# Expert 0's first 256 rows picked by one-hot products, four weight parts moved to GpSimd, and a re-timed order

## What is computed

```python
x = x + tanh(g_xattn[0]) * L0_xattn(layernorm(x), ctx)
x = x + tanh(g_ffn[0])   * L0_ffn(layernorm(x))
x = x + tanh(g_xattn[1]) * L1_xattn(layernorm(x), ctx)
x = x + tanh(g_ffn[1])   * L1_ffn(layernorm(x))
# L1_ffn: 896 tokens, 8 experts, top 2
probs = softmax(x @ gate_w.T); w, idx = top_k(probs, 2); w = w / sum(w)
for each expert e:  g, u = split(x @ gup[e].T)
                    out += combine[:, e] * ((silu(g) * u) @ dn[e].T)
```

## Time and profile before

| what | value |
|---|---|
| time, median of 3 runs (lowest, highest) | 584.78 us (584.68, 585.03) |
| profiled execution, device time | 583.47 us |
| its span, first to last instruction | 581.6 us |
| PE busy | 555.4 us (95%) |
| DVE busy | 408.8 us (70%) |
| ACT busy | 319.4 us (55%) |
| POOL busy | 271.9 us (47%) |
| mean granted TensorE clock | 0.995 |

### The profile page before, as it was taken

One profiled execution on the slowest core, in us unless ns is written; L12 is line 12 of the kernel. 1 busy time (PEld: TensorE's weight loads), 2 busy tenths in 40 slices (PEclk: granted clock), 3 DMA queues, 4 the chain that ended last, 5 costly groups with the idle time before them and its releaser, 6 DMA issues.

```text
span 581.6 us, 13614 instructions
## 1 busy us (share of the span) xinstructions
PE 555.4 (95%) x5542; PEld 477.1 (82%) x5542; DVE 408.8 (70%) x831; ACT 319.4 (55%) x632; POOL 271.9 (47%) x237
## 2 busy tenths in 40 slices
PE   8999999999989999999999999998999999999994
PEld 8776667677657878888888888877899999979994
DVE  7877568578696666777767867767677677746652
ACT  3554555555664665566555556654465656636641
POOL 3755655765740164657567465731203233421424
PEclk9999999999999999999999999999999999999998
DMA  8910840000000000000000000019374567726112
GB/s 259 357 45 2 318 194 3 1 3 2 2 2 1 2 1 2 8 9 17 18 9 18 10 25 1 25 26 414 91 253 149 170 213 253 259 32 236 28 20 26
DMA packets 24091, 50.92 MB, mean 88 GB/s; under 512 B 7072, under 2 KB 17104, under 8 KB 20688
## 3 DMA queue, kind: packets, MB, share of 16 engines
q1 hardware_dynamic: 18560, 45.20, 21.4%
q0 software_dynamic: 4224, 3.70, 3.6%
q10 hardware_dynamic: 1232, 1.01, 0.6%
HBM read 37.89 MB, written 13.31 MB: 88 GB/s over the span
## 4 chain that ended last, share of the span: by engine, by line
PE 81%; DVE 7%; ACT 5%; POOL 4%; issue 2%; DMA 1%; POOLq 0%; DVEq 0%; ACTq 0%
PE ps L59 15%; PE ps L60 14%; PE ps L61 14%; PE ps L607 5%; PE ps L750 4%; PE ps L625 4%; PE ps L768 4%; PE ps L738 4%; ACT P L1642 3%; DVE KN L1140 3%; PE ps L641 3%; PE ps L515 2%; PE ps L816 2%; POOL P L1947 2%; PE ps L522 2%
## 5 line engine op out<-in xcount | busy, mean ns | idle before, releaser
L1947 POOL TENSOR_SCALAR P<-P,rinv 112x487 f32<-112x487 f32 x56 | 88.2, 1588 | 50.9 <-DVE rinv L1183 50.7
L1140 DVE TENSOR_REDUCE KN<-ps 112x4 f32<-112x1500 f32 x32 | 55.0, 1719 | 28.7 <-PE ps L607 28.6
L424 POOL DMA_INDIRECT out<-WS,rows_i x16 | 28.7, 1791 | 92.5 <-ACT WS L1789 89.0
L60 PE MATMUL ps<-XGf,WH 128*128 128x256 f32 x252 | 71.3, 283 | 0.0
L61 PE MATMUL ps<-XGf,WL 128*128 128x256 f32 x252 | 71.3, 283 | 0.0
L59 PE MATMUL ps<-XGf,WH 128*128 128x256 f32 x252 | 71.3, 283 | 0.0
L1886 POOL TENSOR_TENSOR sr<-sv,mhalf 125x32 f32<-125x32 f32 x13 | 70.7, 5435 | 1.1
L1521 DVE TENSOR_TENSOR WL<-WR,WH 128x1024 fp32r<-128x1024 f32 x48 | 57.1, 1219 | 13.6 <-ACT WH L1843 10.0
L1642 ACT ACTIVATE P<-ps 125x1344 f32<-125x1344 f32 x32 | 41.3, 1292 | 32.8 <-PE ps L625 32.8
L1705 ACT ACTIVATE P<-ps,nm 112x487 f32<-112x487 f32 x64 | 41.9, 664 | 31.7 <-DVE nm L1175 31.7
L1843 ACT ACTIVATE WH<-WR 128x1024 fp32r<-128x1024 f32 x48 | 48.7, 1049 | 0.1
(11 more groups left out here) (290 smaller groups left out, 1546.1 us busy)
## 6 DMA issues: line engine op xcount, KB each, us to landing
WR<-in_gupT SPq DMA_DIRECT2D x16, 1024.0 KB, 7.2
WR<-in_dwnT SPq DMA_DIRECT2D x8, 1024.0 KB, 10.3
xs<-ZT SPq DMA_DIRECT2D x14, 516.0 KB, 6.0
CT<-in_ctxT SPq DMA_DIRECT2D x1, 2250.0 KB, 11.1
P<-xs SPq DMA_DIRECT2D x7, 256.0 KB, 10.8
P<-xs SPq DMA_DIRECT2D x9, 128.0 KB, 2.6
Wk<-in_L_xattn_Wk SPq DMA_DIRECT2D x2, 512.0 KB, 11.1
Wv<-in_L_xattn_Wv SPq DMA_DIRECT2D x2, 512.0 KB, 11.1
```

Of the source, the lines that this page charges most:

```text
L60: e.matmul(out, ah, bl, start=False, stop=False)
L1140: e.tensor_reduce(heads(KN[b % 2][0:NQ, 3, :])[:, 4 * k:4 * k + 4, 16], ps[0:NQ, 0:4, 0:NC], AX.X, ALU.max, negate=True).then_inc(s("smax" ...
L1947: e.tensor_scalar(P[:, k, 0:487], P[:, k, 0:487], rinv[:, k:k + 1], None, ALU.mult).then_inc(s("psc"), 1)
```

## The change

Three things are changed.

Expert 0's first 256 rows no longer come from the list in device memory. For each sequence b a matrix PG of 112 tokens x 256 slots is made that holds a one where the token chose expert 0 and stands in that slot. GpSimd makes it for sequences 0 to 6 (stage "pk": a copy of `chosen`, then an is-equal of the slot numbers with `r_u`, times the copy), VectorE for sequence 7, in one operation in the middle of its "rt5". TensorE multiplies XN by PG (stage "pa": two products of 256 columns in full float32 for each sequence, accumulated over the eight in banks 0 and 1); what stands there then is the turned rows. The stage "xin" of expert 0 is only its copy and subtraction now. The two loads of expert 0's rows and the wait for the stores in front of them are gone; SyncE's first load behind the stores is expert 1's. The stores themselves remain, since the other experts and the weights use the list.

The low parts of chunks 0 to 3 of expert 0 are made by GpSimd, those of chunks 4 and 5 as before by VectorE. ScalarE makes all six high parts before it copies the last sequence's turned tokens.

The tables are re-timed, `WARM` is changed, and "xin" of expert 1 stands behind the fourth up unit of expert 0, not the third. The gates' four small operations in sequence 7's chain stand behind the product and the pick.

Of the diff, tables are cut to a line or two:

```diff
+PICK = ((1.67, "pk", 0), (1.95, "pk", 1), (3.34, "pk", 2), (14.8, "pk", 3), (20.7, "pk", 4), (29.03, "pk", 5),
...
-WARM = {("kp", 0, 1, 0): 36, ("spk", 0, 2): 24, ("xt", NB - 1, 3): 18, ("rt4", NB - 1): 26, ("xin", 0): 62,
-        ("up", 0, 0): 10}
+WARM = {("kp", 0, 1, 0): 36, ("spk", 0, 2): 24, ("xt", NB - 1, 3): 18, ("rt4", NB - 1): 10, ("pa", NB - 1): 8,
+        ("up", 0, 0): 8}
...
-            if dc == 2 and x + 1 < NE:
+            if dc == (2 if x else 3) and x + 1 < NE:
                 put("xin", x + 1)
...
+                elif stage == "pa":
+                    b, = i
+                    if b == 0:
+                        w.wait_ge(s("prob"), 2 * NPAIR)
+                    if b < NB - 1:
+                        w.wait_ge(s("pk"), 2 * b + 2)
+                    else:
+                        w.wait_ge(s("picked"), 1)
+                    for k in range(2):
+                        t = e.matmul(ps[:, PAIRS[0][k], 0:256], XN[:, b, k * 128:(k + 1) * 128], PG[:, b, :],
+                                     start=(b == 0), stop=(b == NB - 1))
+                    if b == NB - 1:
+                        t.then_inc(s("xin"), 1)
...
                 at = c + 14
+                if b == NB - 1:
+                    w.wait_ge(s("slots"), 2)
+                    w.wait_ge(s("rchain"), c + 10)
+                    e.scalar_tensor_tensor(PG[:, b, :], slots, r["u"][:, 0:1], chosen[:, b, 0:1].to_broadcast([NQ, 256]),
+                                           ALU.is_equal, ALU.mult).then_inc(s("picked"), 1)
+                    gates(e, w, b, c + 10)
...
-            w.wait_ge(s("scatter"), 32 * NB)
-            for c in range(LATE_LOW, 4):
-                split_low(e, w, 0, c)
...
         def split_low(e, w, x, c):
             cs = slice(c * 1024, (c + 1) * 1024)
             w.wait_ge(s("wh"), 6 * x + c + 1)
+            if (x, c) == (0, 4):
+                w.wait_ge(s("wl"), 4)
...
-            w.wait_ge(s("scatter"), 32 * NB)
-            e.dma_start(XG[:, 1, :], xs[128:256, 0:D]).then_inc(s("xg_first"), 16)
...
+                    e.iota(slots_i, pattern=[[1, 256]], base=0, channel_multiplier=0).then_inc(s("slots"), 1)
+                    w.wait_ge(s("slots"), 1)
+                    e.tensor_copy(slots, slots_i).then_inc(s("slots"), 1)
+                elif stage == "low":
+                    split_low(e, w, *i)
+                elif stage == "pk":
+                    b, = i
+                    w.wait_ge(s("slots"), 2)
+                    w.wait_ge(s("rchain"), RC * b + 14)
+                    e.tensor_copy(R["p2"][:, b, 0:1], chosen[:, b, 0:1]).then_inc(s("pk"), 1)
+                    w.wait_ge(s("pk"), 2 * b + 1)
+                    e.tensor_scalar(PG[:, b, :], slots, R["u"][:, b, 0:1], R["p2"][:, b, 0:1], ALU.is_equal,
+                                    ALU.mult).then_inc(s("pk"), 1)
```

More of the change, by code:

```diff
@@ L142 @@
[L142 to L156, removed]
+EVEN = ((-5.7, "xs1"), (-3.48, "q1", 0), (0.86, "q1c", 0), (3.9, "q1", 1), (5.62, "q1c", 1), (9.87, "k1x", 0),
+        (11.53, "k1xc", 0), (19.54, "k1x", 1), (21.65, "k1xc", 1))
@@ new lines @@
+ODD = ((6.06, "x1c"),)
+PREP1 = ((-6.82, "cs1"), (2.23, "k1", 0), (3.37, "k1c", 0), (2.36, "k1", 1), (5.44, "k1c", 1), (7.38, "k1", 2),
+         (10.55, "k1c", 2), (14.97, "k1", 3), (19.62, "k1c", 3), (19.17, "v1", 0), (18.96, "v1c", 0),
+         (18.89, "v1", 1), (18.58, "v1c", 1), (21.07, "v1", 2), (31.38, "v1", 3), (22.32, "v1c", 2),
+         (33.18, "v1c", 3))
+TAIL1 = ((9.54, "aT"), (13.09, "wo"), (14.24, "res", 3), (14.89, "stats", 3), (16.88, "norm", 3), (20.86, "xt", 3),
+         (19.19, "xtc", 3), (24.49, "rt0"), (21.04, "rt1"), (22.74, "rt2"), (24.47, "rt3"), (27.75, "rt4"),
+         (29.34, "rt5"))
@@ new lines @@
+TAIL_NEXT = ((8.16, "aT"), (12.94, "wo"), (9.94, "res", 3), (21.65, "stats", 3), (22.44, "norm", 3),
+             (25.94, "xt", 3), (24.18, "xtc", 3), (28.72, "rt0"), (30.67, "rt1"), (32.04, "rt2"), (34.39, "rt3"),
+             (55.11, "rt4"), (67.44, "rt5"))
+TAIL_LAST = ((3.1, "rv"), (6.19, "rb"), (4.0, "rbc"), (9.29, "aT"), (9.5, "wo"), (13.18, "res", 3),
+             (14.76, "stats", 3), (27.06, "norm", 3), (28.36, "xt", 3), (47.6, "xtc", 3), (48.16, "rt0"),
+             (48.03, "rt1"), (48.15, "rt2"), (54.71, "rt3"), (54.17, "rt4"), (77.95, "rt5"))
@@ new lines @@
+SPLIT = ((12.04, "split", 0), (21.0, "low", 0), (14.07, "split", 1), (21.32, "low", 1), (21.02, "split", 2),
+         (53.34, "low", 3), (24.66, "split", 3), (36.38, "low", 2), (25.92, "split", 4), (32.12, "split", 5))
+PICK = ((1.67, "pk", 0), (1.95, "pk", 1), (3.34, "pk", 2), (14.8, "pk", 3), (20.7, "pk", 4), (29.03, "pk", 5),
+        (29.24, "pk", 6), (22.54, "pa", 0), (24.2, "pa", 1), (37.14, "pa", 2), (51.21, "pa", 3), (61.73, "pa", 4),
+        (62.6, "pa", 5), (81.66, "pa", 6), (84.72, "pa", 7))
@@ L217, in attention_order @@
         at(d, stage, k)
+    for d, stage, b in PICK:
+        at(pair_at[NPAIR - 4] + d, stage, b)
     for d, stage, c in SPLIT:
@@ L233, in expert_order @@
             put("load", x, c)
-    put("pair", 0)
+    put("pair", 1)
     put("ahead", 0)
-    put("pair", 1)
     for c in range(3):
@@ L402, in build @@
         below, every = PF[0:NQ, 4736:4864], PF[0:NQ, 4864:4992]
+        slots = PF[0:NQ, 4736:4992]
         tri, ones = sb("tri", [NQ, 128], BF), sb("ones", [NQ, 128], BF)
@@ L858, in tensor_experts @@
                 keep_warm(e, w, stage, *i)
-                if stage == "xin":
+                if stage == "xin" and i[0]:
                     x, = i
@@ L864, in tensor_experts @@
                         w.wait_ge(s(f"pair{u % 3}"), u // 3)
+                    w.wait_ge(s(f"xg{j}"), 16 * ((x + 1) // 2))
                     for t_ in range(2):
[L866 to L869, removed]
                         for k in range(2):
@@ L940, in tensor_experts, with rows_in, rows_to @@
                         w.met.pop()
+        def rows_in(x):
+            if x == 0:
+                return ps[:, 0:2, 0:256]
+            return ps[:, PAIRS[pair_use[("xin", x)] % 3][0], :].rearrange("p (k n) -> p k n", k=2)
+        def rows_to(x, v):
+            return XGT[:, x % 2, v, :].rearrange("p (k n) -> p k n", k=2)
         def counts(e, w):
@@ L1385, in vector_route @@
             elif stage == "rt4":
[L1386 to L1392, removed]
+                if b < NB - 1:
+                    gates(e, w, b, c + 9)
             else:
@@ L1412, in vector_route, with gates @@
                     at += 3
+        def gates(e, w, b, at):
+            v2, s1, s2 = (r1[n][:, b:b + 1] for n in ("v2", "s1", "s2"))
+            e.tensor_scalar(s1, v2, 1.0, None, ALU.add).then_inc(s("rchain"), 1)
+            w.wait_ge(s("rchain"), at + 1)
+            e.reciprocal(s2, s1).then_inc(s("rchain"), 1)
+            w.wait_ge(s("rchain"), at + 2)
+            e.tensor_scalar(XN[:, b, D:D + 1], s2, tg[0:NQ, 3:4], None, ALU.mult).then_inc(s("rchain"), 1)
+            e.scalar_tensor_tensor(XN2[b][:, D:D + 1], v2, s2, tg[0:NQ, 3:4], ALU.mult,
+                                   ALU.mult).then_inc(s("rchain"), 1)
         def first_of(e, w, at, eq, mx, oh):
```

28 lines of the change are left out of this document (10 added, 18 removed).

## The result

The changed kernel takes 595.98 us (median of 4 runs, 594.94 to 596.49), the kernel before 584.89 us (4 runs beside them): ratio 1.0192, 95% interval 1.0180 to 1.0204. It is 11.1 us slower, where 4.05 us less had been forecast. The profiled execution took 596.49 us, the slowest of its four, its span is 594.7 us, TensorE's mean granted clock 0.986; so the two traces lie 13.1 us apart (594.7 - 581.6) where the medians lie 11.1 apart.

What follows compares the result with a forecast made beforehand. TensorE bounds the kernel, but a store-and-load chain through other engines sets the first gate; TensorE's queue replaces it. -4.6 + 0.35 + 0.2 = -4.05 us: profiled 583.47 becomes 579.4, median 580.7, range 579.1 to 582.3 (0.60).

Steps and rivals of the forecast that it cites:

- VectorE beside GpSimd: Last routing beside GpSimd's last two low parts: VectorE's operations slow a little, counted as 0.2 us lost.
- The first two end by 404.7: GpSimd's first two low parts end before sequence 7's variance comes at about 405.4, so no wait.
- Fewer fills leave no longer idle stretch, so I count nothing.: TensorE's clock in the passage to the first gate stays at 1.00, its 2.4 GHz level; no cost counted.
- Rival 2: VectorE's two-SBUF-input routing operations each wait for a whole GpSimd low part: +5.0 us, 585.5 us; chance 0.08.
- GpSimd's own prices: On GpSimd: 1.15 us a pick, 2.95 a low part; four picks end at 396.7, sequence 6's root at 397.6.
- rival 1: GpSimd's picks hold sequence 6: four end 2.7 us later, and everything behind its root too, 583.4 us; chance 0.15.
- hidden, barely: Four GpSimd picks fit ahead of sequence 6's root, done at 397.6 against 397.53 before; margin 0.1 us.
- TensorE's queue, gate at 415.8: From sequence 7's projection (401.8), TensorE's queued work of 13.2 us sets the first gate, 4.6 us earlier.
- Expert 1's turn, 0.35 us: Behind the gate, expert 1's turn stands only one down unit ahead of its first use: 0.35 us lost, once.
- The tables: Second attention layer's stages change places by one or two: at most 1.7 us either way, nothing counted.
- I am wrong if TensorE idles for more than 1 us between 400 and the gate: Stated sign of failure, beside the gate moving by 4 to 5 us without the end moving.

Runs made afterwards that it cites:

- the probe: Computation left out, zeros output: three equal GpSimd instructions run while VectorE does one operation; its copy took 2.01 us beside low parts, 0.43 by itself.
- the low parts placed: Against the kernel with low parts on VectorE (581.95 us): sequence 3's pick behind sequence 6's root, third and fourth low parts moved on VectorE; 579.65 us, 0.9920.

## Why the prediction was wrong

- **VectorE beside GpSimd, 0.2 us: the step that failed.** VectorE waited 10.9 us behind GpSimd's low parts, and with what follows that cost 14.0 us. The row that I leaned on, an operation that passed in 0.47 us inside scalings, was true of scalings, as the probe shows (0.48 for the same form), and r_e's 0.592 is what a scaling holds in its first 0.51 us (the r_e of 326.47 began 0.1 us into one); but a low part is another form. The trace of before does have thirteen GpSimd operations of two inputs and 5.43 us each, and an operation of VectorE with two SBUF inputs that began 0.06 us into one passed in its usual time (the rows below). So neither two inputs nor the length of GpSimd's instruction decides it alone, and what does no run here shows. No row of before had the low part's form, so the price should have been bounded by the whole run.

```profile
69.20 5.43 POOL L1886 TENSOR_TENSOR sr<-sv,mhalf 125x32 f32<-125x32 f32 x1
```
```profile
69.26 0.49 DVE L1234 SCALAR_TENSOR_TENSOR X<-tt,tg,X 112x256 f32<-112x256 f32 x1
```

- **"The first two end by 404.7", "no wait".** They ended at 405.17. I asked only whether GpSimd was done in time, not what its being busy does to VectorE.
- **"Fewer fills leave no longer idle stretch, so I count nothing."** The fills weren't at fault, but VectorE's waits left longer idle stretches, and the clock then cost 5.1 us: 6.66 and 4.80 us without products were followed by mean clocks of 0.53 and 0.68, while 1.35 us (low parts on VectorE) were followed by 1.00.
- **Rival 2, chance 0.08,** was right in kind and sign, and so is the rule of the Trainium skill beside it, but for the two points above. Its places were off by one: the first two low parts met sequence 7's copy, not sequence 6's routing, the last two r_t of sequence 6, not r_e of sequence 7. Its time, 585.5, was 10.5 us short: it gave each operation one low part (5.3 us of waits), left out the copy, which has one input, and had no clock.
- **GpSimd's own prices.** A pick takes 1.22 us and comes every 1.47, not 1.15; sequence 6's root was done at 398.99, not 397.6. Moving one pick behind the root is worth 1.48 us, so rival 1 (2.7 us) held too, by half its size, beside rival 2: "hidden, barely" was no margin. A low part takes 2.32 us, under my 2.95. On TensorE a pick takes 0.86 to 0.95 us at full clock, taken as 0.91: right.
- **TensorE's queue, gate at 415.8.** Right to 1 us once the two faults are out: with the low parts placed, the projection starts at 401.33 (401.8 forecast), the gate at 414.83, and 579.65 us stand against 580.7.
- **Expert 1's turn, 0.35 us.** About right: expert 2's turn starts 27.13 us behind the gate (459.63 - 432.50), 26.52 before (446.93 - 420.41), 0.61 more, of which 0.18 are lost inside the gate (its ten products take 1.79 us for 1.61) and some 0.4 at expert 1's first up unit. No wait for the stores or a load was seen, as forecast. **The tables** are nothing: up to the cast the kernels differ by -0.6 to 0.3 us.
- **"I am wrong if TensorE idles for more than 1 us between 400 and the gate"** named the right sign. Another 0.4 us between the last product and the end of the span has no cause shown.

## What to carry to other kernels

Work that is moved to an idle GpSimd can hold VectorE: before moving it, ask which VectorE operations with two SBUF inputs, copies or column operations run beside it, and price each at the rest of GpSimd's queued run, not at a share of bandwidth, until a probe has timed that very form of GpSimd operation beside them. If such an operation stands in TensorE's path, add what the clock loses behind the gap. A subtraction that VectorE does in 1.22 us at a place of its own choice can be cheaper than the same one "for nothing" on GpSimd in 2.32.

## What the runs showed of the hardware

- A VectorE operation that began under a pick or scaling of GpSimd waited for every low part queued behind: 3.62, 5.92, 8.22 us for one, two, three. Begun under a low part it waited for that one alone (2.41).
- One-input VectorE operations wait too: the 112 x 512 copy (2.01 for 0.43) and the column subtraction of 8 columns (1.75 for 0.23). A maximum and an operation with an input in PSUM passed.
- GpSimd's column operations, picks and scalings, let VectorE through but for their first 0.39 and 0.51 us (0.43 to 0.76 for the copy, by where it began); so did its two-input operation of 125 x 32 (0.49 us for VectorE's inside one of 5.43). Its 128 x 1024 copy held VectorE nearly to its end (0.70 for 0.43).
- VectorE's low parts hold GpSimd too: a pick of 1.22 us took 3.15 beside two of them.
